# Nine propagation steps of a graph network: one panel in seven summed from rows fetched by index

## The chip, the core and the metric

One core of a Trainium2 chip runs the kernel: TensorE (PE) multiplies, VectorE (DVE), ScalarE (ACT) and GpSimd (POOL) work on tiles, and SyncE (SP) issues most DMAs, which run on 16 DMA engines. The metric is the time of one execution in microseconds of device time; less is better. In the rows PEld is PE's load of a weight block, and a name with a q behind it (SPq, PEq) is an engine's sequencer.

## What is computed

Four graph layers on 6250 nodes with 96 features and 100,000 edges (src, dst): attention, a softmax sum, ten steps of propagation (APPNP) and two graph convolutions. The change touches the third:

```python
# h: [6250, 96]; w = rsqrt(deg(src) * deg(dst)) for each edge
def spmm(feat):
    msg = feat[dst] * w[:, None]
    return segment_sum(msg, src, num_segments=6250)
out = h
for _ in range(10):
    out = spmm(out) * 0.9 + h * 0.1
```

## The kernel before

Nodes are cut into 49 tiles of 128. Once, in the attention stage, the kernel builds the adjacency as counts of edges, one byte (fp8) each, and stores it in HBM both ways round: `adjacency` and `adjacency_t`. For a tile of nodes (by src), a *panel* is its 128 columns of counts against all 6250 nodes (by dst), 49 blocks of 128 x 128 (128 rows of 6400 bytes). The sum for one tile is 49 matmuls (L1795), each with a block of counts as weights and 192 columns moving: 96 of the features in f16 and 96 of their remainder, so that the result is near f32. The features live in SBUF in two arrays, Ua (shown as `y`) and Ub (`u2b`), one read in a step and the other written.

A step has 7 *bodies* of 7 panels. Panel r of a body sits in ring slot r and sums into PSUM bank r. The queues:

- **SP** (`loads`, L1783) loads panel r of the next body as soon as PE is done with panel r of this one (`done`), so loads run a whole body ahead.
- **PE** (`products`) waits for the bank (`free`) and the slot (`ring_in`), then does 49 matmuls. In a step's first panel it waits before block 42 until all 49 tiles of this step's features are there (`u_ready`), so the last seven tiles of the step before may still be under way.
- **DVE** and **ACT** (`rows`, `copies`) turn each bank into the next features: ACT L1819, DVE L1804 and L1807, ACT L1822, DVE L1811, ACT L1825, each waiting for the one before.
- **POOL** does nothing in this stage.

The first step and the four pairs of steps after it are loops over bodies, the last step is unrolled. In the last step's first body the DVE also makes `w_squares`, for which PE waits (L1740).

Ahead of it lies the softmax layer (`softmax_dense`), whose 7 blocks of 7 panels are summed by L1443 with 385 columns. There DVE first makes the inputs (`product`, `remainders`, seven times) and then, block by block, empties the banks (L1521 and L1522, then the division L1529 to L1539). PE starts on a bank of the next block when DVE has emptied it.

The lists behind the counts: in the bucket stage edges are sorted to `k.slots`, for each group of 256 nodes by dst (25 groups) and each tile by src there are 128 slots, each of which holds at most one edge. Four planes hold src's position in the tile (plus one; zero for an empty slot) and three parts of dst's place in the group.

Of the kernel before, what the change touches and what calls it, by code (L numbers as in the profile page):

```python
# [5 lines left out]
ALU = mybir.AluOpType  # L6
# [34 lines left out]
BODIES = TILES // RING  # L41
SLOT = RING * BANK * GROUP
# [82 lines left out]
def signals(k):  # L125
# [17 lines left out]
    k.codes, k.decoded, k.planes = k.sig("codes"), k.sig("decoded"), k.sig("planes")  # L143
    k.base1, k.full_s, k.full_ps, k.filled_s = (k.sig(x) for x in ("base1", "full_s", "full_ps", "filled_s"))
# [809 lines left out]
def attention_and_adjacency(k, ctx):  # L954
# [392 lines left out]

    norm = Norm(k)
    vector(), gpsimd(), paired(pe, tensor_step), scalar(), paired(sp, sync_step, SP_LAG)
    for e in (v, a, pe, pool, sp):  # L1350
        for b in range(2):
            e.wait_ge(k.col_out[b].sem, k.col_out[b].at(PAIRS - 1 if b < last_tiles else PAIRS - 2, 15))
# [24 lines left out]
def dense_signals(k):  # L1377
    k.ring_in = [k.sig(f"ring{r}") for r in range(RING)]
    k.used, k.free, k.done = k.sig("used", RING - 1), k.sig("free", RING), k.sig("done", RING)
    k.w2_set, k.unit_root, k.shrunk = (k.sig(x) for x in ("w2_set", "unit_root", "shrunk"))  # L1380
# [8 lines left out]
    k.unit, k.unit_ps, k.per_unit = (k.sig(x) for x in ("unit", "unit_ps", "per_unit"))  # L1389
    k.x_out = k.sig("x_out")  # L1390

# [83 lines left out]

def softmax_dense(k, ps, bank, Y, Ua):
# [5 lines left out]
    with ExitStack() as ctx:  # L1482
# [7 lines left out]
        blocks = Blocks(k, ps, [U], cols)  # L1490
        folded = Folded(k, bank, k.T, k.wl[0:1], k.agg,
# [5 lines left out]
        def vector():  # L1497
# [15 lines left out]
            k.res.base += BODIES  # L1513
            for i in range(BODIES):
                v.wait_ge(k.agg.sem, k.agg.at(i))
# [135 lines left out]
        scalar(), vector(), scalar_sums(), tensor(), blocks.sync(early=1), first_loads()  # L1651
        for x in (v, a, k.pool):
            x.wait_ge(k.u_ready.sem, k.u_ready.at(TILES))
# [108 lines left out]
def appnp_and_convolutions(k, ctx, ps, bank, Ua, out):  # L1762
# [4 lines left out]
    v, a, pe, sp = k.v, k.a, k.pe, k.sp  # L1767
# [11 lines left out]
    def loads(n):  # L1779
        for r in range(RING):  # L1780
            sp.wait_ge(k.done.sem, k.done.at(RING * n["at"] + r + 1 - RING))
            k.settle(sp)
            sp.dma_start(k.ring[r][:, 0:WIDE], k.t_d[RING * n["body"] + r, :, :]).then_inc(k.ring_in[r].sem, 16)  # L1783

    def products(n):
        for r in range(RING):
            pe.wait_ge(k.free.sem, k.free.at(RING * n["at"] + r + 1 - RING))
            pe.wait_ge(k.ring_in[r].sem, k.ring_in[r].at(16 * n["at"] + 16))
            k.settle(pe)
# [36 lines left out]

    def numbers(eng):


        def bodies(step, U, Un, first=0):  # L1830
            if eng is pe:
                pe.wait_ge(k.u_ready.sem, k.u_ready.at(TILES * step + TILES - RING))
                k.settle(pe)
            with eng.Fori(first, BODIES) as i:
                yield {"step": step, "body": i, "at": step * BODIES + i, "this": U, "next": Un}
# [499 lines left out]
```

## Time and profile before

| | |
|---|---|
| median of 3 runs | 3998.27 us (3998.01 to 3999.06) |
| profiled execution, first to last instruction | 3998.4 us |
| PE busy | 3854.9 us, 96% |
| DVE, ACT, POOL busy | 44%, 33%, 15% |
| mean granted TensorE clock | 0.989 |
| propagation, L1795 from its loops on | 1594.4 to 3561.2 us |
| DMA engines, 2000 to 2200 us | 0.60 of their time, 204 GB/s |

The profile comes from one execution that was recorded; its span is the number in the second row, and what lies around it does not show beside the runs (0.1 us). A matmul's mean time in groups (246 ns) is its time in a pipeline; how fast they follow each other is read from a chain's length over its count.

### The profile page before, as it was taken

What the parts mean: (1) busy time and instruction counts of PE and PEld (TensorE: products, weight loads), DVE (VectorE), ACT (ScalarE), POOL (GpSimd) and SP (SyncE); (2) the same over time, 40 slices, a digit from 0 to 9 for tenths busy, and PEclk for the clock granted to TensorE, in tenths of its full rate; (3) what the DMA queues carried; (4) which work ended last, traced back from release to release, by engine and by line L of the source; (5) the groups of instructions that cost most, each with busy time, mean ns of one, the idle gap of its engine ahead of it and who ended that gap; (6) DMA issues with size and microseconds to landing.
All of it is one profiled execution on the core that took longest, in us unless ns stands there. A gap on an engine that the chain in (4) does not pass through costs nothing.

```text
span 3998.4 us, 124106 instructions
## 1 busy us (share of the span) xinstructions
PE 3854.9 (96%) x46183; PEld 3660.9 (92%) x46183; DVE 1769.7 (44%) x4393; ACT 1314.9 (33%) x3901; POOL 586.7 (15%) x714
## 2 busy tenths in 40 slices
PE   3889999999989999999999999999999998999999
PEld 2679999999956667999999999999999998999999
DVE  8999999999973324222222222222222222331111
ACT  1248888888871111222222122222222221111110
POOL 1016666666630000000000000000000000000000
PEclk9989999999989999999999999999999999999999
DMA  1039999889963333665665665656656665667775
GB/s 41 3 79 235 232 238 233 233 235 237 231 189 111 111 111 111 220 202 202 205 204 201 203 204 203 200 203 205 201 201 204 204 200 177 202 219 213 209 214 156
DMA packets 438001, 747.73 MB, mean 187 GB/s; under 512 B 197331, under 2 KB 330579, under 8 KB 437840
## 3 DMA queue, kind: packets, MB, share of 16 engines
q1 hardware_dynamic: 433346, 744.61, 61.1%
q8 instruction: 126, 2.06, 0.2%
q10 hardware_dynamic: 4494, 0.77, 0.1%
q14 instruction: 35, 0.29, 0.0%
HBM read 621.82 MB, written 83.32 MB: 176 GB/s over the span
## 4 chain that ended last, share of the span: by engine, by line
PE 91%; DVE 6%; ACT 1%; issue 1%; DMA 0%; ACTq 0%; DVEq 0%; SPq 0%; POOL 0%; POOLq 0%
PE sum L1795 49%; PE sum L1443 19%; PE pk L1182 10%; PE pr L1205 7%; PE pq L1194 3%; PE pc L1218 2%; DVE onerank L799 2%; PE l L475 1%; DVE bt L771 1%; DVE prodb L788 1%; DVE vals L781 1%; PE l L459 0%; DMA X<-in_x_dram 0%; DVE H L283 0%; PE sum L1622 0%
## 5 line engine op out<-in xcount | busy, mean ns | idle before, releaser
L1795 PE MATMUL sum<-u2b,ring 128*128 128x192 f16 x12005 | 994.1, 246 | 0.0
L1795 PEld LDWEIGHTS sum<-u2b,ring 128*128 128x128 fp8e4 x12005 | 993.1, 98 | 0.3
L1795 PE MATMUL sum<-y,ring 128*128 128x192 f16 x11662 | 962.9, 246 | 0.0
L1795 PEld LDWEIGHTS sum<-y,ring 128*128 128x128 fp8e4 x11662 | 962.2, 98 | 0.0
L1804 DVE TENSOR_TENSOR z<-lo,sum 128x96 f32<-128x96 f32 x441 | 112.2, 254 | 983.1 <-ACT lo L1819 982.8
L1182 PE MATMUL pk<-kv,hT 128*128 128x192 f16 x4900 | 485.6, 246 | 2.0 <-DVE hT L1074 2.0
L1443 PE MATMUL sum<-u,ring 128*128 128x385 f16 x2401 | 404.6, 329 | 12.4 <-ACT u L1585 12.4
L1182 PEld LDWEIGHTS pk<-kv,hT 128*128 128x128 f16 x4900 | 409.9, 99 | 2.4 <-DVE hT L1074 2.3
L1443 PEld LDWEIGHTS sum<-u,ring 128*128 128x128 fp8e4 x2401 | 236.0, 98 | 174.2 <-issue 13.6
L1264 ACT ACTIVATE kvs<-pk 128x384 f32<-128x384 f32 x735 | 301.0, 437 | 112.5 <-PE pk L1182 92.0
L1819 ACT ACTIVATE lo<-sum 128x96 f32<-128x96 f32 x441 | 110.1, 250 | 649.3 <-PE sum L1795 648.9
L1205 PE MATMUL pr<-wv,hs_wide 128*128 128x101 f32 x2450 | 321.2, 278 | 1.6 <-POOL wv L1135 1.6
L1130 POOL TENSOR_SCALAR sc<-sc,bound 128x20 f32<-128x20 f32 x245 | 270.2, 1103 | 276.5 <-DVE sc L1058 276.5
L1205 PEld LDWEIGHTS pr<-wv,hs_wide 128*128 128x128 f32 x2450 | 292.8, 192 | 1.9 <-POOL wv L1135 1.9
L1135 POOL TENSOR_TENSOR wv<-kvs,wv 128x480 f32<-128x480 f32 x245 | 246.5, 1006 | 204.2 <-DVE hd L1105 150.1
L1443 PE MATMUL sum<-u2b,ring 128*128 128x192 f16 x2401 | 203.0, 246 | 0.7 <-ACT u2b L1981 0.7
L1443 PE MATMUL sum<-y,ring 128*128 128x192 f16 x2401 | 202.2, 246 | 0.0
L1443 PEld LDWEIGHTS sum<-u2b,ring 128*128 128x128 fp8e4 x2401 | 199.1, 98 | 1.1 <-ACT u2b L1981 1.0
L1443 PEld LDWEIGHTS sum<-y,ring 128*128 128x128 fp8e4 x2401 | 199.0, 98 | 0.1
L1237 ACT ACTIVATE row<-pc 128x512 uint16<-128x512 f32 (+1 forms) x343 | 185.8, 546 | 0.7
L1254 ACT ACTIVATE hs_wide<-hs 128x640 f32<-128x640 bf16 x245 | 180.0, 735 | 0.0
L1051 DVE TENSOR_TENSOR qk<-pq,kvs 128x480 f32<-128x480 f32 x245 | 160.1, 653 | 42.9 <-ACT kvs L1264 42.9
(254 smaller groups left out, 3363.3 us busy)
## 6 DMA issues: line engine op xcount, KB each, us to landing
ring<-adjacency_t SPq DMA_DIRECT2D x490, 800.0 KB, 4.3
ring<-adjacency SPq DMA_DIRECT2D x147, 896.0 KB, 4.9
rows<-slot_rows_d SPq DMA_DIRECT2D x249, 320.0 KB, 4.0
adjacency<-row SPq DMA_DIRECT2D x49, 800.0 KB, 4.4
adjacency_t<-col SPq DMA_DIRECT2D x49, 800.0 KB, 4.6
col<-row SPq DMA_TRANSPOSE x245, 4.1
out_dram<-X SPq DMA_DIRECT2D x6, 336.0 KB
slot_rows_d<-T SPq DMA_DIRECT2D x2, 240.0 KB
```

The costliest lines, as they stand in the source:

```text
L1051: v.tensor_tensor(qk[i][:].rearrange("p (g d) -> p g d", d=D), pq[i][:, 0:CHUNK * D].rearrange("p (g d) -> p g d", d=D), kv[i][:, :, 0:D], ...
L1130: pool.tensor_scalar(sc[i][:], sc[i][:], k.bound[:, 0:1], k.bound[:, 1:2], ALU.min, ALU.max).then_inc(k.clipped.sem, 1)
L1135: pool.tensor_tensor(wv[i][:, :, 0:D].rearrange("p g (h d) -> p g h d", d=DH), kv[i][:, :, D:2 * D].rearrange("p g (h d) -> p g h d", d=DH ...
L1182: t = pe.matmul(pk[n][:, place:place + 2 * D], hT[i][:, 1 + m, g, :], k.kv[:, 2 * (g0 + g) + m, part, :], start=m == part == 0, stop=m == ...
L1194: t = pe.matmul(pq[i][:, g * D:(g + 1) * D], hT[i][:, 0, g, :], q2[b][:, part, :], start=part == 0, stop=part == 1)
L1205: t = pe.matmul(pr[:, 0:AV], hs_wide[e % HOMES][:, g, :], wv[i][:, g, :], start=g0 + g == 0, stop=g0 + g == GROUPS - 1)
L1237: a.activation(flat(row[b][:, g:g + count, :]), pc[u % 2][:, 0:count * P], ACT.Copy, accum_out=rowsum[:, bass.ds(X * (2 * UP) + u, 1)]).th ...
L1254: a.activation(flat(hs_wide[e % HOMES][:]), hs[e % 2][:].rearrange("p g a t -> p (g a t)"), ACT.Copy).then_inc(k.wide.sem, 1)
L1264: a.activation(flat(kv[i][:, 2 * n:2 * n + count, :]), pk[n][:, 0:count * 2 * D], ACT.Copy).then_inc(k.kv_out.sem, 1)
L1443: t = pe.matmul(self.ps[j][:, 0:self.cols], w[:, q, (j + odd) // 2, :, (j + odd) % 2], U[:, r * RING + q, 0:self.cols], start=r == q == 0, ...
L1795: m = pe.matmul(ps[r][:, 0:2 * D], w[:, t // 2, :, t % 2], n["this"][:, t, 0:2 * D], start=t == 0, stop=t == TILES - 1)
L1804: v.tensor_tensor(z[:, j, :], lo[:, j, :], ps[j][:, 0:D], ALU.add).then_inc(k.free.sem, 1)
```

## The change

For panel 6 of each body, in steps 2 to 10, the 49 blocks of counts are replaced by 25 pairs of a list and a one-hot. For each group of 256 nodes there is a list of 128 node numbers (`k.index`), one a slot, and a matrix of 128 slots by 128 columns that is 1 where the slot's edge belongs (`hots_d`, 3200 bytes a row). PE then does 25 matmuls (L1898 of the new kernel) with the one-hots as weights and the fetched rows moving. The rows, 128 of 384 bytes for each list, are fetched by GpSimd with one indirect DMA a list from a table of the features in HBM (`u_d`, one for each of Ua and Ub), into two buffers `got` in turn. What was added for it:

- SP stores the slots to HBM (`slots_d`) before attention.
- In the softmax stage POOL reads the planes back, works out the indices (`indices`) and stores one-hots (`store`), which DVE builds (`one_hots`), seven of 3200 elements, before it empties the first banks.
- In propagation SP stores each body's new features to the table (`publish`) behind the next body's loads, and POOL waits for all seven stores of a step before its first gather.
- The loops over bodies on SP, PE and POOL become one loop over four pairs of steps with 14 bodies written out; DVE's and ACT's stay.

```diff
+        sp.dma_start(k.slots_d, k.slots[:].rearrange("p i t g -> p (i t g)")).then_inc(k.slots_kept.sem, 16)
...
+    def one_hots(self, j):
+        v.wait_ge(k.listed.sem, k.listed.at(2))
+        for b in range(j * BODIES, (j + 1) * BODIES):
+            if b >= 2:
+                v.wait_ge(k.hot_out[b % 2].sem, k.hot_out[b % 2].at(16 * (b // 2)))
+            v.tensor_tensor(self.hots[b % 2][:], under(k.count1[:], GROUPS), over(self.which[:, b, :], P),
+                            ALU.is_equal).then_inc(k.hot_built.sem, 1)
+    def store(self):
+        for b in range(PICKED_TILES):
+            pool.wait_ge(k.hot_built.sem, k.hot_built.at(b + 1))
+            pool.dma_start(k.hots_d[b, :, :], flat(self.hots[b % 2][:])).then_inc(k.hot_out[b % 2].sem, 16)
...
+            if r >= PICKED and n["turn"]:
+                sp.dma_start(k.ring[r][:, 0:GROUPS * P], k.hots_d[(r - PICKED) * BODIES + n["body"], :, :]).then_inc(k.ring_in[r].sem, 16)
...
+    def publish(at, rows_of, h, b):
+        sp.wait_ge(k.u_ready.sem, k.u_ready.at(TILES + RING * at + RING))
+        sp.dma_start(k.u_d[h][RING * b * P:RING * (b + 1) * P, :].rearrange("(t p) d -> p t d", p=P),
+                     rows_of[:, tiles_of(b), 0:2 * D]).then_inc(k.u_out[h].sem, 16)
+    def gathers(n):
+        if b == 0:
+            pool.wait_ge(k.u_out[n["table"]].sem, k.u_out[n["table"]].at(16 * BODIES * n["times"]))
+        for j in range(PICKS):
+            h, at = (PICKS * n["turn"][0] + j) % 2, j * BODIES + b
+            pool.wait_ge(k.done.sem, k.done.at(RING * (n["at"] - 2 // PICKS) + PICKED + j + 1))
+            for g in range(GROUPS):
+                pool.indirect_dma_start(got[h][:, g, :], None, k.u_d[n["table"]], bass.IndirectOffsetOnAxis(
+                    ap=k.index[:, at, g:g + 1], axis=0)).then_inc(k.got[h].sem, 16)
...
+            if r >= PICKED and n["turn"]:
+                pe.wait_ge(k.got[turn % 2].sem, k.got[turn % 2].at(16 * GROUPS * (seen + turn // 2 + 1)))
+                for g in range(GROUPS):
+                    m = pe.matmul(ps[r][:, 0:2 * D], w[:, g, :], got[turn % 2][:, g, :],
+                                  start=g == 0, stop=g == GROUPS - 1)
```

On PE, two bodies in the last step read as follows before, each bank `sum_r` with its ring slot:

```order
L1795 MATMUL sum_4<-u2b,ring_4 128x192 x49
L1795 MATMUL sum_5<-u2b,ring_5 128x192 x49
L1795 MATMUL sum_6<-u2b,ring_6 128x192 x49
L1795 MATMUL sum_0<-u2b,ring_0 128x192 x49
L1795 MATMUL sum_1<-u2b,ring_1 128x192 x49
```

And in the change, in the unrolled pair of steps:

```order
L1908 MATMUL sum_4<-u2b,ring_4 128x192 x49
L1890 REGISTER_ALU
L1908 MATMUL sum_5<-u2b,ring_5 128x192 x49
L1890 REGISTER_ALU
L1894 ISA
L1898 MATMUL sum_6<-got0,ring_6 128x192 x25
L1890 ISA
L1891 ISA
L1908 MATMUL sum_0<-u2b,ring_0 128x192 x49
```

The seventh bank takes 25 matmuls from `got0` (then `got1`) in place of 49 from the features in SBUF. On POOL, whose program had no row for this stage, the loop now begins so, the gathers of body 0 and body 1 of a step:

```order
L2006 UNCONDITIONAL_BRANCH
L2006 ISA
L1882 ISA
L1885 DMA got0<-u_rows_d1,index 128x192 x25
L1882 ISA
L1885 DMA got1<-u_rows_d1,index 128x192 x25
```

Between two bodies' gathers stands only the wait for a buffer. On DVE, at the end of the softmax layer's inputs, before:

```order
L1566 TENSOR_TENSOR T<-T,u1 128x672
L1568 TENSOR_TENSOR y1<-y1,u1 128x672
L1521 TENSOR_TENSOR dn1<-lo1,sum_0 128x192
L1522 TENSOR_SCALAR ideg<-sum_0 128x1
L1521 TENSOR_TENSOR dn1<-lo1,sum_1 128x192
```

and in the change:

```order
L1644 TENSOR_TENSOR T<-T,u1 128x672
L1646 TENSOR_TENSOR y1<-y1,u1 128x672
L1533 TENSOR_TENSOR hots0<-count1,which 128x3200
L1533 TENSOR_TENSOR hots1<-count1,which 128x3200
L1533 TENSOR_TENSOR hots0<-count1,which 128x3200
L1533 TENSOR_TENSOR hots1<-count1,which 128x3200
L1533 TENSOR_TENSOR hots0<-count1,which 128x3200
L1533 TENSOR_TENSOR hots1<-count1,which 128x3200
L1533 TENSOR_TENSOR hots0<-count1,which 128x3200
L1599 TENSOR_TENSOR dn1<-lo1,sum_0 128x192
L1600 TENSOR_SCALAR ideg<-sum_0 128x1
```

Seven comparisons now stand between the last remainder and the first sum.

## Rows read from the trace of the kernel before

**Rows 1.** The page: the chain that ended last, shares by line.

```profile
PE sum L1795 49%; PE sum L1443 19%; PE pk L1182 10%; PE pr L1205 7%; PE pq L1194 3%; PE pc L1218 2%; DVE onerank L799 2%; PE l L475 1%; DVE bt L771 1%; DVE prodb L788 1%; DVE vals L781 1%; PE l L459 0%; DMA X<-in_x_dram 0%; DVE H L283 0%; PE sum L1622 0%
```

**Rows 2.** Chain in order of time: start us, length us, what.

```profile
1594.39 1782.75 PE sum L1795 x21609
3388.70 172.48 PE sum L1795 x2058
```

**Rows 3.** Windows: PE, PEld, DVE, ACT, POOL busy; granted clock; DMA share; GB/s.

```profile
2000.00:2200.00 200.00, 200.00 (x2427) 200.00 (x2425) 41.00 (x148) 40.53 (x149) 0.00 (x0) 1.00 0.60 204
```

**Rows 4.** Timeline of ACT, one panel sum and the next: start us, length us.

```profile
2200.80 0.25 ACT L1819 ACTIVATE lo<-sum 128x96 f32<-128x96 f32 x1 [1.52 <-PE sum L1795]
...
2203.03 0.28 ACT L1825 ACTIVATE y<-r 128x96 f32 x1 [0.70 <-DVE r L1811]
2204.84 0.25 ACT L1819 ACTIVATE lo<-sum 128x96 f32<-128x96 f32 x1 [1.53 <-PE sum L1795]
```

**Rows 5.** Chain at the start of the last step.

```profile
3377.23 0.26 ACT lo L1888
...
3387.95 0.74 PE l L1740 x2
```

**Rows 6.** Windows behind that idle stretch: PE busy, clock, DMA share, GB/s.

```profile
3390.00:3395.00 5.00, 5.00 (x38) 0.59 0.01 3
3395.00:3400.00 5.00, 5.00 (x64) 1.00 0.48 164
```

**Rows 7.** Line 1783, the ring loads: ns min/median/max on SP, us to landing.

```profile
L1783 SPq DMA_DIRECT2D ring<-adjacency_t x483: 327/333/343, 1587.7 to 3533.0; - x161
...
DMA to landing us min/median/max: 4.0/4.3/11.7
```

**Rows 8.** DMA list of the whole span: the smallest loads.

```profile
es<-in_src_dram SPq DMA_DIRECT2D x25, 18.0 KB, 1.7
```

**Rows 9.** Lines by form, GpSimd: count, busy us, mean ns.

```profile
L1135 POOL TENSOR_TENSOR wv<-kvs,wv 128x480 f32<-128x480 f32 x245 | 246.5, 1006 | 204.2 <-DVE hd L1105 150.1 <-ACT wv L1244 51.1 <-issue 0.2
```

**Rows 10.** Line 1130 on GpSimd: ns min/median/max.

```profile
L1130 POOL TENSOR_SCALAR sc<-sc,bound x245: 352/1537/1540, 273.6 to 1126.1; 128x20 f32<-128x20 f32 x123
```

**Rows 11.** DMA in propagation, 2000 to 2200 us: packets, MB, share of 16 engines.

```profile
q1 hardware_dynamic: 7149, 40.74, 60.3%
```

**Rows 12.** DMA in attention, 300 to 330 us.

```profile
DMA packets 7796, 7.23 MB, mean 241 GB/s; under 512 B 6206, under 2 KB 6206, under 8 KB 7792
...
q1 hardware_dynamic: 7792, 7.18, 95.4%
```

**Rows 13.** Timeline where the softmax sums begin, 1189 to 1262 us.

```profile
1191.64 32.58 PE L1443 MATMUL sum<-u,ring 128*128 128x385 f16 x196 [0.20 <-ACT u L1585]
...
1194.50 0.86 DVE L1566 TENSOR_TENSOR T<-T,u 128x672 f32<-128x672 f32 x1
...
1195.39 0.86 DVE L1568 TENSOR_TENSOR y<-y,u 128x672 f32<-128x672 f32 x1
...
1201.61 0.35 DVE L1521 TENSOR_TENSOR dn<-lo,sum 128x192 f32<-128x192 f32 x1 [5.35 <-ACT lo L1597]
...
1205.40 0.36 DVE L1529 TENSOR_SCALAR e<-dn 128x384 f32<-128x384 f32 x1
...
1209.83 0.56 DVE L1539 TENSOR_TENSOR T<-dn,H 128x384 f32<-128x384 f32 x1
```

**Rows 14.** Lines by form, VectorE: the comparison that builds bt.

```profile
L771 DVE TENSOR_TENSOR bt<-number,tiles 128x1764 bf16<-128x1764 bf16 x25 | 26.8, 1071 | 0.0
```

**Rows 15.** Timeline at 1141 us, while GpSimd works too.

```profile
1131.90 10.63 POOL L1340 TENSOR_TENSOR X<-X,T 128x672 f32<-128x672 f32 x6
...
1140.99 2.25 DVE L1566 TENSOR_TENSOR T<-T,u 128x672 f32<-128x672 f32 x1
```

**Rows 16.** Chain after 3600 us, where PE runs unrolled code.

```profile
3612.02 16.17 PE sum L1443 x196
```

**Rows 17.** Instruction DMA from 3600 to 3998 us: packets, MB, share.

```profile
q8 instruction: 39, 0.64, 0.6%
```

More of the change, by code:

```diff
@@ L1379, in dense_signals @@
     k.used, k.free, k.done = k.sig("used", RING - 1), k.sig("free", RING), k.sig("done", RING)
-    k.w2_set, k.unit_root, k.shrunk = (k.sig(x) for x in ("w2_set", "unit_root", "shrunk"))
+    k.w2_set, k.unit_root, k.shrunk = Again(k, k.counted, GROUPS), Again(k, k.before, GROUPS), Again(k, k.same, 2 * GROUPS)
     k.u_set, k.exps, k.prods, k.hi, k.res, k.lo, k.hi2, k.res2, k.lo2 = (
@@ L1651, in softmax_dense @@
         scalar(), vector(), scalar_sums(), tensor(), blocks.sync(early=1), first_loads()
+        picked.indices(), picked.store(), picked.end()
         for x in (v, a, k.pool):
@@ L1762, in appnp_and_convolutions @@
 def appnp_and_convolutions(k, ctx, ps, bank, Ua, out):
-    v, a, pe, sp = k.v, k.a, k.pe, k.sp
+    v, a, pe, pool, sp = k.v, k.a, k.pe, k.pool, k.sp
+    got = [k.buf(ctx, f"got{i}", [P, GROUPS, 2 * D], F16) for i in range(2)]
     Ub = k.buf(ctx, "u2b", [P, TILES, 2 * D], F16)
@@ L1850, in last_products, with sync, publish_before, gpsimd @@
                 unit.sums()
+    def sync():
+        for b in range(1, BODIES):
+            loads({"body": b, "at": b, "turn": None})
+            publish(b - 1, Ub, 1, b - 1)
+        with sp.Fori(0, last // 2) as s:
+            for n in pair(s):
+                loads(n)
+                publish_before(n)
+        for n in last_each():
+            loads(n)
+            if n["body"] == 0:
+                publish_before(n)
+    def publish_before(n):
+        h, b = n["table"], n["body"]
+        if b == 0:
+            publish(n["at"] - 1, n["this"], h, BODIES - 1)
+        else:
+            publish(n["at"] - 1, Ua if n["this"] is Ub else Ub, 1 - h, b - 1)
+    def gpsimd():
+        with pool.Fori(0, last // 2) as s:
+            for n in pair(s):
+                gathers(n)
+        for n in last_each():
+            gathers(n)
     def last_rows():
-        for n in last_numbers():
+        for n in last_each():
             b = n["body"]
@@ L1880, in last_copies @@
     def last_copies():
-        for n in last_numbers():
+        for n in last_each():
             b = n["body"]
@@ L1896, in last_copies @@
                 unit.root()
-    for n in numbers(sp):
-        loads(n)
-    for n in numbers(pe):
-        products(n)
+    sync(), tensor(), gpsimd()
     for n in numbers(v):
@@ L1905, in appnp_and_convolutions @@
         copies(n)
-    for n in last_numbers():
-        loads(n)
-    last_products(), last_rows(), last_copies()
+    last_rows(), last_copies()
     of_all = STEPS * BODIES
@@ L2016, in dense_layers @@
         Ua = Y[:].bitcast(F16)
+        k.index = k.buf(ctx, "index", [P, PICKED_TILES, GROUPS], I32)
         ps, bank = [k.bank(ctx, f"sum_{j}") for j in range(RING)], k.bank(ctx, "l")
```

116 lines of the change are left out of this document (99 added, 17 removed).

## Prediction

> **What bounds the kernel now.** I read the chain of work that ended last first. Propagation's matmul line L1795 alone is 49% of the span, the largest item by far [rows 1]. The chain in order of time then shows 21,609 of its matmuls in 1782.75 us without a piece of anything else between them [rows 2]. That is 82.5 ns a block, 4.04 us for a panel of 49 blocks, 28.3 us for a body and 198.1 us for a step. A window of 200 us inside has PE and its weight loads busy for all 200, VectorE and ScalarE for 41 each, GpSimd for nothing, and the DMA engines for 0.60 of their time [rows 3]. So every block taken from PE there is worth 82.5 ns, as long as nothing that PE needs comes later than PE.
>
> Two things are to be seen beside that. The work behind a panel is a chain on ScalarE and VectorE: it starts at 2200.80, its last copy ends at 2203.31, and the next begins at 2204.84 when the next panel is done [rows 4]. It is 2.51 us of 4.04, so it has slack. And PE's only idle stretch in propagation is in the last step, from 3377.2 to 3387.95 [rows 5]. After it the granted clock is 0.59 in the window from 3390 to 3395, where 38 matmuls ran, and 1.00 in the next, where 64 did [rows 6]: the lower level, 1.2 GHz, and then 2.4 again. The 2058 matmuls behind the gap took 172.48 us, 83.8 ns each, and 169.8 would have done [rows 2]. So a wait of 10.7 us cost another 2.7 us in clock.
>
> **The change, part by part.** Removed: in 63 bodies (nine steps of seven) the seventh panel needs 25 blocks in place of 49. 63 x 24 x 82.5 ns = 124.7 us, or 13.9 us a step. This is certain; the rest eats from it.
>
> Added in each step, the gathers. They read a table in HBM that holds all 49 tiles, so none of a step's gathers can start before the last tile of the step before is copied, stored and landed. Let S be the moment when PE ends a step. Panel 5 ended 2.06 us (25 blocks) earlier, its chain of 2.51 us ends at S + 0.5, that of panel 6 at S + 3.1 [rows 4]. (PE needs these tiles at block 42 of the next panel, S + 3.5: still in time, with 0.4 us left where there was 0.9.) SP issues the store in 0.33 us, and I let it land like a ring load, whose least is 4.0 us [rows 7]: S + 7.5. GpSimd starts at S + 7.6. The 25 gathers of body 0 take 25c, c being the time that GpSimd needs for one, and the last lands 1.7 us after its issue, as the smallest loads do [rows 8]. PE, meanwhile, has six full panels, 24.3 us. So PE waits 7.6 + 25c + 1.7 - 24.3 = 25c - 15.0 us at body 0's seventh panel. For the seventh body the same account is 7.6 + 175c + 1.7 - (24.3 + 6 x 26.3) = 175c - 172.8, since gathers run on behind each other, two bodies deep. PE's wait in a step is the larger of the two. They cross at c = 1.05.
>
> No row shows c. From below it is SP's issue of a load to 128 partitions, 0.33 us [rows 7]; from above a whole small load from issue to landing, 1.7 us, as if no two overlapped [rows 8]. I take 1.0 us: a software engine builds addresses for 128 partitions here, and the nearest row on that engine is its two-input operation, 1006 ns [rows 9]. It could be disturbed: another GpSimd instruction takes 352 ns at best and 1537 at the median beside a busy VectorE [rows 10], but VectorE is busy only a fifth of the time in propagation [rows 3]. At c = 1.0 the wait is 10.0 us, and by the gap above 2.7 us of clock come with it: 12.7 a step, 114.3 us in nine.
>
> The SBUF page of the Trainium skill (SBUF — State Buffer, SBUF: two separate sides) gives about 620 ns for a GpSimd-issued DMA alone, and 3100 ns beside a VectorE operation that holds the shared port. By the first figure as an estimate for c the wait would be 0.5 us and the kernel at about 3905; no run here shows it, and it is a plain DMA, not one that reads indices. The second figure would be the rival of a GpSimd that is the bound, and is kept out by the code, where propagation's VectorE operations take two inputs.
>
> DMA load: a body's 3200 fetched rows of 384 bytes and 896 stored ones. A packet of the ring loads takes 0.27 us of an engine (0.603 x 16 x 200 us over 7149 [rows 11]). In attention 7792 packets, 6206 of them under 512 bytes, took 458 engine-us in 30 us [rows 12]. If the 1586 others cost 0.27 each, 0.005 us is left for a small one; if all cost the same it is 0.059. With 0.059 the rows add 242 us to the 421 that 16 engines have in a body of 26.3, 0.57 on top of the rings' 0.60: over the limit. In proportion to bytes (384 of 6400) a row costs 0.02, which adds 0.19. I take this one, between the ends and in keeping with the bytes, at no cost to PE, and keep the other as a rival.
>
> Added once, the one-hots. Seven comparisons of 3200 elements stand on VectorE between the last remainder, which ends at 1196.25, and the first sum at 1201.61 [rows 13]. At one element a cycle (384 elements 0.56 us, 672 elements 0.86: 1.04 ns each [rows 13]) one is 3.5 us; at the rate of the bf16 comparison, 1764 in 1.07 us [rows 14], 1.8. I take 3.5, the output being bytes. Two buffers, and a store that lands about 5 us after a buffer is built (GpSimd's 1.0 and 4.0 as above): the pace becomes 8.5 us a pair, and VectorE is free after 28.9 us, at 1225.2. PE needs bank 0 at 1207.8, two panels of 8.1 us behind 1191.64 [rows 13]. It gets it at 1225.7: 17.9 us. Bank 4 waits behind four sums and the 5 us of division that begin at 1205.40 in the trace of before [rows 13]: 2.6 us more. With 2.7 of clock: 23.2. Bounds: 4 (1.8 us each and no wait for stores) and 30. PE is the bound all through this stage, so nothing gives it back.
>
> Small ones. The slots' store, 1.28 MB, goes in front of SP's queue where attention begins and the engines are busiest: 0 to 3.5 us, I take 1.8. The index arithmetic on GpSimd falls under the chain on which PE waits there; beside GpSimd one VectorE operation took 2.25 us [rows 15] in place of 0.86 [rows 13], so 2 us. PE's loop is now 14 unrolled bodies. Unrolled code runs at 82.5 ns as well, 196 matmuls in 16.17 us [rows 16], while 39 instruction fetches pass [rows 17]; the branch back comes at a step's start, under the wait for gathers. Nothing for it; up to 10 us if that cover is gone.
>
> **Sum** against the profiled execution, whose span of 3998.4 us is within 0.2 of the median of 3998.27: 3998.4 - 124.7 + 114.3 + 23.2 + 1.8 + 2.0 = **4015 us**, +0.4%.
>
> **The rivals.** With F = 3900.7 for all but the gathers, the time is F + 9 x (wait + 2.7).
>
> *Gathers are cheap (c below 0.89): faster.* The place is body 0's seventh panel and the price 225 us per microsecond of c. At c = 0.8 the wait is 5.0: 3970. At 0.6 it is gone: 3901. It decides from c = 0.93, where the sum is nil. For it: GpSimd's small operation takes 352 ns undisturbed [rows 10] and SP's issue 333 [rows 7]. Against: those do no address work in software. Chance 0.36. The Trainium skill's figure of 620 ns, cited above, stands on this side.
>
> *GpSimd becomes the bound (c above 1.06): slower by 1% and more.* At 1.1 the seventh body waits 19.7: 4102. At 1.2, 37.2: 4260. At 1.7, 124.7: 5048. For it: the 1537 ns in [rows 10], and that 25 gathers must fit in 26.3 us with nothing over. Chance 0.23.
>
> *The DMA engines become the bound.* At a load of 1.17 a body takes 30.8 us, 2.5 more than before: 3998.4 + 27.0 + 63 x 2.5 = 4183. For it: the 95% in [rows 12]. Against: ring loads there and here are large packets with room beside them [rows 3]. Chance 0.04.
>
> *My forecast*, c from 0.89 to 1.06: 3990 to 4040. Chance 0.37. It rests on a GpSimd instruction over 128 partitions being worth a microsecond, as in [rows 9].
>
> **How the numbers follow.** About 0.2%, 8 us, is what a measurement of this kernel can tell from no change. Faster is c below 0.89: 0.36. Within 8 us is c from 0.89 to 0.96, a wait of 7.2 to 9.0 us: 0.12. The rest is slower, 0.52. The range leaves out c above 1.17 (4213) and keeps the case without any wait: 3900 to 4215. The forecast's own range is 3990 to 4040.
>
> **What would show it.** Right: line L1898's matmuls, 1575 of them, with PE idle some 10 us before those of body 0 of each step, released by the gathers, almost nothing before the other six, a clock of about 0.6 behind each wait, gathers a microsecond apart on GpSimd, and a PE gap near 1208 us of some 18 us. Wrong: PE waiting at every seventh panel (GpSimd too slow), a step of 184 us without a gap (c small), or waits at L1908 for ring loads (DMA full). The prediction is most sensitive to c: 0.1 us of it is 22 us of time, and above 1.05, 157.

## The result, and the profile of the changed kernel

The changed kernel takes 5836.84 us (5834.33 to 5838.57), the kernel before 3998.18 us in the same comparison: a ratio of 1.460, interval 1.458 to 1.462. The prediction was 4015 us with a range from 3900 to 4215. The profiled execution has a span of 5836.9 us at a mean granted clock of 0.82.

The page of the changed kernel: the shares of the chain that ended last by engine and by line (answers to [rows 1]), and the costliest groups.

```profile
PE 67%; issue 27%; DVE 5%; ACT 1%; DMA 0%; ACTq 0%; DVEq 0%; SPq 0%; POOL 0%; POOLq 0%
PE sum L1908 36%; PE sum L1456 12%; PE pk L1186 7%; PE pr L1209 5%; PE sum L1898 2%; PE pq L1198 2%; PE pc L1222 1%; DVE onerank L803 1%; PE l L479 1%; DVE bt L775 0%; DVE prodb L792 0%; DVE vals L785 0%; DVE hots L1533 0%; PE l L463 0%; DMA X<-in_x_dram 0%
...
L1885 POOL DMA_INDIRECT got<-u_rows_d,index x1575 | 1495.2, 949 | 2634.5 <-PE sum L1898 1131.9
L1908 PE MATMUL sum<-u2b,ring 128*128 128x192 f16 x10290 | 1085.6, 262 | 846.6 <-issue 845.3
...
L1908 PE MATMUL sum<-y,ring 128*128 128x192 f16 x10290 | 1033.3, 258 | 691.1 <-issue 690.4
```

What the reader expects after the prediction, PE waiting for fetched rows at L1898, isn't there at all. In its place PE stands idle for 1536 us in front of the matmuls of the six *other* panels, and what ended that time is "issue": it waited for nothing that the profile shows. It is GpSimd that waits for PE. The timeline of PE, one body and the start of the next (L1908: a panel of counts; L1898: the fetched panel), shows the form of it:

```profile
2444.14 2.23 PE L1898 MATMUL sum<-got,ring 128*128 128x192 f16 x25
2446.20 5.72 PE L1908 MATMUL sum<-y,ring 128*128 128x192 f16 x66
2452.17 0.24 PE L1908 MATMUL sum<-y,ring 128*128 128x192 f16 x1 [0.25 <-issue]
...
2469.15 0.32 PE L1908 MATMUL sum<-y,ring 128*128 128x192 f16 x1 [1.08 <-issue]
2471.25 0.32 PE L1908 MATMUL sum<-y,ring 128*128 128x192 f16 x1 [1.78 <-issue]
2473.35 0.32 PE L1908 MATMUL sum<-y,ring 128*128 128x192 f16 x1 [1.78 <-issue]
...
2482.48 18.89 PE L1908 MATMUL sum<-y,ring 128*128 128x192 f16 x200 [1.08 <-issue]
2501.21 2.23 PE L1898 MATMUL sum<-got,ring 128*128 128x192 f16 x25
```

When PE ends L1898 at 2446.2, GpSimd starts the next 25 gathers (one body's 25 in a row are called a *burst* here). PE runs 66 more matmuls at full speed, and then from 2452 to 2482 it issues few: first three or four at a time, then single ones, 0.7 to 2.1 us apart in this body, until the burst is over. Then 200 follow in 18.9 us. A body takes 57.1 us (2444.14 to 2501.21) in place of 26.3. I call this a *slow phase*. Windows of the changed kernel, with the columns of [rows 3]: 200 us of propagation, a piece between bursts and one within a burst.

```profile
2000.00:2200.00 200.00, 130.28 (x1363) 118.57 (x1363) 24.44 (x89) 23.80 (x89) 67.35 (x72) 0.78 0.46 140
2427.00:2446.00 19.00, 19.00 (x220) 18.88 (x219) 3.90 (x14) 3.80 (x14) 0.00 (x0) 0.94 0.56 181
2454.00:2474.00 20.00, 4.42 (x19) 1.74 (x19) 0.86 (x3) 0.82 (x3) 15.12 (x17) 0.56 0.33 81
```

1363 matmuls in 200 us stand against 2427 before. In the burst there are 19 in 20 us, the DMA engines are two thirds idle, and the clock has fallen to 0.56. The gaps come before the fall: from 2446 to 2452 the granted clock is 1.00, and the matmul at 2452.17, behind the first gap, still lasts 0.24 us; those from 2469 on last 0.32. So the low clock doesn't start the slow phase.

### The profile page after: what moved, and what is told of

Same layout as the page of the kernel before. It is cut to its first block, busy times and chain, and to the rows that moved or that the text cites. A ratio compares the mean times of both kernels' runs of the same rounds, so it can differ in the third digit from the quotient of the medians.

```text
span 5836.9 us, 121842 instructions
## 1 busy us (share of the span) xinstructions
PE 4137.6 (71%) x44671; PEld 3658.3 (63%) x44671; DVE 1793.2 (31%) x4400; ACT 1313.7 (23%) x3901; POOL 2074.9 (36%) x2311
## 4 chain that ended last, share of the span: by engine, by line
PE 67%; issue 27%; DVE 5%; ACT 1%; DMA 0%; ACTq 0%; DVEq 0%; SPq 0%; POOL 0%; POOLq 0%
PE sum L1908 36%; PE sum L1456 12%; PE pk L1186 7%; PE pr L1209 5%; PE sum L1898 2%; PE pq L1198 2%; PE pc L1222 1%; DVE onerank L803 1%; PE l L479 1%; DVE bt L775 0%; DVE prodb L792 0%; DVE vals L785 0%; DVE hots L1533 0%; PE l L463 0%; DMA X<-in_x_dram 0%
## 5 line engine op out<-in xcount | busy, mean ns | idle before, releaser
L1885 POOL DMA_INDIRECT got<-u_rows_d,index x1575 | 1495.2, 949 | 2634.5 <-PE sum L1898 1131.9
L1908 PE MATMUL sum<-u2b,ring 128*128 128x192 f16 x10290 | 1085.6, 262 | 846.6 <-issue 845.3
L1908 PEld LDWEIGHTS sum<-u2b,ring 128*128 128x128 fp8e4 x10290 | 921.5, 103 | 1006.1 <-issue 995.6
L1908 PE MATMUL sum<-y,ring 128*128 128x192 f16 x10290 | 1033.3, 258 | 691.1 <-issue 690.4
L1908 PEld LDWEIGHTS sum<-y,ring 128*128 128x128 fp8e4 x10290 | 904.0, 102 | 816.2 <-issue 808.1
L1456 PE MATMUL sum<-u,ring 128*128 128x385 f16 x2401 | 405.9, 329 | 29.9 <-DVE ideg L1600 16.5
L1134 POOL TENSOR_SCALAR sc<-sc,bound 128x20 f32<-128x20 f32 x245 | 235.6, 962 | 285.2 <-DVE sc L1062 285.2
L1456 PE MATMUL sum<-u2b,ring 128*128 128x192 f16 x2401 | 203.0, 246 | 0.7 <-ACT u2b L2136 0.7
L1456 PE MATMUL sum<-y,ring 128*128 128x192 f16 x2401 | 202.2, 246 | 0.0
L1456 PEld LDWEIGHTS sum<-u2b,ring 128*128 128x128 fp8e4 x2401 | 199.1, 98 | 1.1 <-ACT u2b L2136 0.9
L1456 PEld LDWEIGHTS sum<-y,ring 128*128 128x128 fp8e4 x2401 | 199.0, 98 | 0.1
```

Source lines behind the costliest of these rows:

```text
L1134: pool.tensor_scalar(sc[i][:], sc[i][:], k.bound[:, 0:1], k.bound[:, 1:2], ALU.min, ALU.max).then_inc(k.clipped.sem, 1)
L1456: t = pe.matmul(self.ps[j][:, 0:self.cols], w[:, q, (j + odd) // 2, :, (j + odd) % 2], U[:, r * RING + q, 0:self.cols], start=r == q == 0, ...
L1885: pool.indirect_dma_start(got[h][:, g, :], None, k.u_d[n["table"]], bass.IndirectOffsetOnAxis(ap=k.index[:, at, g:g + 1], axis=0)).then_in ...
L1908: m = pe.matmul(ps[r][:, 0:2 * D], w[:, t // 2, :, t % 2], n["this"][:, t, 0:2 * D], start=t == 0, stop=t == TILES - 1)
```

## The experiments

Eighteen runs were made, of seventeen kernels, each beside the kernel before. The letters of the theories hold within one batch only; each is told where it first stands. "The change" in an expectation is the changed kernel. The edits are shown in part; `...` marks what is left out.

**First batch: which part of the change does it.** Two parts were added to the kernel before, alone and together: gathers that nobody reads (20 a body, of 128 neighbouring rows), and PE's code of steps 2 to 9 written out body by body, as the change has it. The fourth is the change without its gathers. The edit of the gathers and that of the fourth:

```
+    def fetch(at, turn, seen):
+        h = turn % 2
+        pool.wait_ge(k.done.sem, k.done.at(RING * (at - 2) + RING))
...
+        for g in range(20):
+            pool.indirect_dma_start(got[h][:, g, :], None, k.u_table, bass.IndirectOffsetOnAxis(
+                ap=index[:, g:g + 1], axis=0)).then_inc(k.got[h].sem, 16)
+        pool.wait_ge(k.got[h].sem, k.got[h].at(16 * 20 * (seen + turn // 2 + 1)))
...
-            for g in range(GROUPS):
-                pool.indirect_dma_start(got[h][:, g, :], None, k.u_d[n["table"]], ...
+            pool.memset(got[h][:, 0:1, 0:2], 0.0).then_inc(k.got[h].sem, 1)
```

Gathers beside PE's loop:

> The kernel before with GpSimd gathers beside it: 20 indirect DMAs of 128 rows of 384 bytes for each body of steps 2 to 10, paced by the same signal as in the change, and read by nobody; PE keeps its loop over one body and all its 49-block panels. Theory A (PE's instruction fetch does not get through while GpSimd runs gathers; code that loops in place needs none): 3998 to 4015 us, PE at 82.5 ns a block. Rival B (gathers slow PE itself, by SBUF or semaphore traffic): PE falls back in each burst of 25 us as in the change, above 5000 us. Rival C (the DMA engines are too busy, ring loads land late): PE waits for ring loads at L1795, 4050 to 4400 us.

PE's code written out, no gathers:

> The kernel before with PE's loop written out to 14 bodies, as the change has it, and no gathers. Theory A: code that is only run straight on is fetched in time, so 3998 to 4010 us, with a microsecond or so for each of the three branches back. Rival D (unrolled PE code is slow in itself in this stage): PE drops to single matmuls as in the change, above 5000 us. B and C: no change, 3998 us.

Both:

> Both together: PE's loop written out to 14 bodies and the 20 gathers a body beside it, still read by nobody. Theory A: PE loses most of each burst (20 gathers at 1.25 us are 25 us, of which some 20 are lost): 4900 to 5400 us, with single matmuls 1 to 2.5 us apart and no 16 KB instruction packet inside the bursts. Rival B and C: the same time as the run with gathers and the looped code. Rival D: the same time as the unrolled code alone.

The change without its gathers:

> The change with its gathers left out: GpSimd only counts its semaphore up, and PE multiplies the one-hots with a buffer of zeros, so that a seventh of the sums is left out. Everything else stays: stores to the table, one-hots, slots, unrolled code. It measures all terms of the prediction but the gathers: 3900.7 us by its sum. Theory A: 3895 to 3915. If PE's unrolled code or the new stores were what costs, it stays above 4500.

Measured: 4004.43 us (ratio 1.0013, 1.0003 to 1.0022) for gathers beside the loop; 4008.55 (1.0024, 1.0014 to 1.0034) for written-out code; 4019.71 (1.0050, 1.0034 to 1.0066) for both; 3915.27 (0.9789, 0.9773 to 0.9806) for the change without gathers. So every theory that blamed the mere pair of gathers and written-out code seemed to fall. It had not: these four ran on chip 1, on which no kernel had slow phases, and in the third batch a pair of the same kind (47 of its rows are row 64) has them on chip 14. What stays is that the change without its gathers, which leaves a seventh of the sums out, is 83 us faster than the kernel before.

**Second batch: the rows.** The lists have empty places (some 46 of 128), and all of a list's empty places name one row. Perhaps these reads of one row disturb. The edits: `k.index` from an iota (rows in order, so that the seventh panels sum other rows); `part` plus (row p - 64) times (place is empty) (own rows); PE's steps 2 to 9 as a loop with one buffer `got`; and the run with both parts, with 47 of its 128 rows the same.

> The change as it is, but every gather takes 128 neighbouring rows of the table (group g the rows from 128g) in place of the rows that the lists name, so the seventh panels sum other rows than the reference. Theory H (in the change about 46 of a list's 128 places are empty and all name one row, and these reads of one row hold up the fetching of TensorE's written-out instructions): the single matmuls 0.7 us apart vanish, GpSimd's 25 x 1.25 us a body bound the steps, 3915 + 9 x 48.7 = about 4353 us (4300 to 4450). Theory S (what slows TensorE is not in the rows but in the rest of the change: SyncE's and GpSimd's code written out beside TensorE's, or TensorE's wait on the fetched rows): as the change, 5837 us (5700 to 5900). Theory R (any rows that aren't in order, not one row above all): as H here.

> The change with one thing more: each empty place of a list names a row of its own (row p of the group's 256) in place of the one that all of them name; its factor in the one-hots is zero, so the sums stay what they are. Theory H (the reads of one row): about 4353 us (4300 to 4450). Theory R (rows out of order): 5837 us (5700 to 5900), since 82 of 128 rows are scattered as before. Theory S: 5837 us.

> The change with TensorE's code of steps 1 to 8 as a loop over bodies again and one buffer of fetched rows in place of two (a loop can't name them in turn). The burst for a body now begins when the seventh panel before it is done and the panel waits for its landing: a body is 31.25 + 2.7 landing + 2.1 for the 25 matmuls = 36.3 us, against 26.3 of TensorE alone, so 3915 + 63 x 10 = about 4550 us (4450 to 4700) under every theory that puts the slow matmuls down to fetching written-out instructions (H, R, and S as far as it is TensorE's own code); the last step, still written out, may be slow by itself (+150). If TensorE is slow for another reason (power, the reading of the fetched rows, banks): each of the 294 matmuls of the six panels is as slow as now, and a body is 31 + 26 us or more: 5840 us and up.

> The kernel before with TensorE's steps written out and 20 gathers a body beside them that nobody reads (the earlier run of this kind took 128 neighbouring rows and 4020 us): now 81 of a gather's 128 rows are every third of 256, and the other 47 are one row, as in the lists of the change. Theory H: TensorE's fetches are held up for the 25 us of each 28 that gathers run, over 4900 us. Theory R: the same, over 4900. Theory S: 4020 us (4010 to 4040).

Measured: rows in order 4314.07 us (1.079, 1.0772 to 1.0808), own rows 4315.72 (1.0787, 1.0769 to 1.0805), the loop with one buffer 4735.13 (1.1839, 1.1819 to 1.1859), one row in 47 places 4020.13 (1.0052, 1.0036 to 1.0069). The first three were free of slow phases, so theory H looked confirmed; but the fourth, which should have shown it, was free of them too. H was in doubt, and the third said that the change's own rows did no harm beside a loop.

**Third batch: which row.**

```
-    pool.tensor_scalar(place[:], place[:], 243.0, 1.0, ALU.min, ALU.mult)
+    # in words: row 3p up to place p = 81, else row 64 (six instructions)
...
-        pool.iota(self.own[:], [[0, GROUPS]], base=-P // 2, channel_multiplier=1, ...
+        pool.memset(self.own[:, 0:GROUPS - 1], 179.0).then_inc(k.listed.sem, 1)
```

> As the run with TensorE's steps written out, 20 gathers that nobody reads and 47 of 128 rows the same (4020 us), but the one row is row 64 of the group's 256, the very row that the change's empty places name, in place of row 243. Theory A (it matters where in memory the one row lies): TensorE waits for its instructions as in the change, over 4500 us. Theory B (the rows alone don't do it; it takes something else of the change with them, such as the stores of the table, SyncE's written-out code or TensorE's wait for the fetched rows): 4020 us (4010 to 4030).

> The change, but the empty places name row 243 of their group (in the last group row 123) in place of row 64; still one row for all of a list's empty places. Theory A (where the one row lies): 4316 us, as with a row for each place (4300 to 4500). Theory B (that it is one row, together with something else of the change): 5837 us (5700 to 5900).

> The change, but of the empty places those above 104 name row 65 and those below row 64, so that some 23 places name one row in place of 46. If the number of reads of one row in one gather matters and each costs its time, the slow phases get shorter: about halfway between 4316 and 5837, 5000 us (4600 to 5500). If there is a threshold: 4316 or 5837.

Measured: 5431.71 (1.3579, 1.3556 to 1.3602), 5815.12 (1.4537, 1.4513 to 1.4562) and 5808.7 (1.4524, 1.4499 to 1.4548). The two rows, expected at 5000 if the number of reads counts, cost as much as one. Neither theory explains all three together with the batch before: row 243 is harmless in one kernel (4020) and not in another (5815). What this batch did give is the effect without the rest of the change: slow phases beside gathers that nobody reads. Windows from 2000 to 2200 us of the run with row 243 and of that with row 64:

```profile
2000.00:2200.00 200.00, 196.75 (x2353) 196.10 (x2351) 39.82 (x144) 39.16 (x144) 128.48 (x136) 0.98 0.75 232
```

```profile
2000.00:2200.00 200.00, 129.84 (x1313) 114.46 (x1311) 21.99 (x80) 21.77 (x80) 75.29 (x80) 0.78 0.42 131
```

**Fourth batch: loop, nine rows, row 127.** The same edits with PE's loop restored, with `own = p / 6 - 13.667`, and with 127 for 64.

> The run with 47 of 128 rows at row 64 that took 5432 us, but TensorE's steps 1 to 8 as the kernel before has them, a loop over bodies; the gathers are the same and nobody reads them. Theory F (what these reads hold up is the fetching of TensorE's written-out instructions): the slow phases vanish in steps 1 to 8, about 4015 us; the last step has its own written-out code and may keep its slow phases (up to 7 x 25 = 175 us more, 4190). Theory G (TensorE's matmuls or its reading of memory are slowed themselves): about 5430 us as with written-out steps.

> The change, but the some 46 empty places of a list name nine neighbouring rows (64 to 72 of the group, about six places each) in place of one. If only many reads of the very same row do it: 4316 us, as with a row for each place. If it is that these places all name rows close together: 5837 us. Two rows of 23 each gave 5809 us. I expect something between, near 4316 (4300 to 5000).

> As the run with TensorE's steps written out and the same row 64 in 47 of 128 places of 20 gathers that nobody reads (5432 us), but the one row is 127 of the group. With row 243 it was 4020 us. If row 243 was spared because of where it lies, any other row may be slow or not: 4020 or about 5430. If row 243 was spared because it was the row that follows the last of the listed ones (3 x 81), so that the reads never go back: 5430 us here, since row 127 lies below the last.

Measured: 5465.42 (1.3668, 1.3645 to 1.3691), 5835.45 (1.4594, 1.4569 to 1.4618), 5467.68 (1.3674, 1.3651 to 1.3697). The nine rows, expected near 4316, missed. The first is the important one. PE's code is the loop of the kernel before, and the slow phases are there at the same size (the expectation of Theory G). From 2000 to 2200 us the DMA list of that run has 2 packets in the queue `q8 instruction`, that of the run with written-out code and row 64 has 11 for about as many matmuls (1276 against 1313), so the loop isn't fetched anew in each turn. Theory F, that fetching of written-out code is held up, fell. GpSimd's first gather and PE in that kernel, from the panel's end that released the burst:

```profile
2105.45 0.95 POOL L1936 DMA_INDIRECT got<-u_rows_d,index  x1 [27.45 <-PE sum L1799]
```

```profile
2104.74 5.47 PE L1799 MATMUL sum<-u2b,ring 128*128 128x192 f16 x64
2110.48 0.24 PE L1799 MATMUL sum<-u2b,ring 128*128 128x192 f16 x1 [0.27 <-issue]
...
2120.50 0.32 PE L1799 MATMUL sum<-u2b,ring 128*128 128x192 f16 x1 [1.81 <-issue]
2123.28 0.32 PE L1799 MATMUL sum<-u2b,ring 128*128 128x192 f16 x1 [2.47 <-issue]
...
2133.78 22.70 PE L1799 MATMUL sum<-u2b,ring 128*128 128x192 f16 x254 [1.78 <-issue]
```

**Fifth batch: a version meant to win.** Own rows; body 0 of a step takes counts throughout, and bodies 1 to 6 fetch 22 lists and keep the last five blocks of counts, so that GpSimd's 6 x 22 x 1.25 us fit into a step. The second has PE's bodies 1 to 6 as a loop of pairs.

```
+                for g in range(LISTS):
+                    m = pe.matmul(ps[r][:, 0:2 * D], w[:, g, :], got[turn % 2][:, g, :], start=g == 0, stop=False)
...
+                for t in range(2 * LISTS, TILES):
+                    m = pe.matmul(ps[r][:, 0:2 * D], w[:, t // 2, :, t % 2], n["this"][:, t, 0:2 * D],
+                                  start=False, stop=t == TILES - 1)
```

> A version that should beat both: a row for each empty place; in six of a step's seven bodies (not the first, which would wait for the whole table) 22 of the 25 lists are fetched and the five last blocks of counts stay. GpSimd needs 22 x 1.25 = 27.5 us for a body and has seven bodies' time (about 188 us) for six; the last burst ends at about 6.5 + 165 + 2.7 = 174 us of a step, TensorE comes to it at 185: no wait. Saved: 54 x 22 x 82.5 ns = 98.0 us, against 124.7 in the run without gathers (3915 us), and the gathers beside written-out code cost 11 us in an earlier pair of runs: 3915 + 26.7 + 8 = about 3950 us (3935 to 3975). If GpSimd still binds: over 4000.

> The same with TensorE's bodies 1 to 6 of a step as a loop over pairs of bodies (the two buffers in turn), its first body written out. If fewer instructions to fetch are worth what the kernel before's steps written out cost (10 us): about 3942 us (3930 to 3965). If the loop of two bodies (642 matmuls and as many loads) is fetched anew in each turn, the same as written out, 3950.

Measured: 5374.37 (1.3438, 1.3416 to 1.3461) and 5378.34 (1.3447, 1.3425 to 1.3469): both missed, with slow phases in both, though no two empty places share a row. With this, no rule by rows was left.

**The two last: rows against code, and chip against kernel.** The kernel with own rows again, with one constant changed (`base=0, channel_multiplier=0`), so that instruction for instruction it is the 4316 us kernel and fetches the rows of the 5837 us kernel:

> The kernel with a row for each empty place (4316 us), instruction for instruction, but one constant is other: the empty places all name row 64 of their group again, so that the gathers fetch exactly the rows that the change fetches (5837 us), by the code of the kernel that took 4316. Theory R (the rows that are fetched decide): 5837 us (5750 to 5850). Theory P (the rows are all the same to it, and what decides is something that a few instructions more or less on GpSimd ahead of the gathers shift): 4316 us (4300 to 4350).

Measured: 4332.2 us (1.0838, 1.082 to 1.0856), free of slow phases. The rows don't decide. Theory P, the placing of GpSimd's code, would remain, but it doesn't sort the runs either: counted in GpSimd instructions ahead of the first gather, the change plus 0, 1, 4 and 5 gave slow, free, free, slow, and plus 0 (the loop with one buffer) free, plus 4 (22 lists) slow. Nor does the place of the buffers: the version with row 243 (5815, slow) allocates the same buffers as the own-rows kernel (4316, free). What does sort them is the chip that timed them, and the last run asked for that with the kernel of 5374 us:

> The version with 22 lists (5374 us, timed on chip 9), the same kernel once more. Theory C (what slows TensorE during bursts of gathers goes with the chip, not with the kernel: all kernels with gathers timed on chips 1 and 11 were free of it, all timed on chips 9 and 14 had it, whatever their rows and code): on chip 1 or 11 3950 us (3935 to 3975), below the kernel before; on chip 9 or 14 5374 us; on another chip one of these two. Theory K (it goes with the kernel): 5374 us on every chip.

Measured: 5375.41 us (1.3438, 1.3416 to 1.3461), on chip 10, one not used so far: as Theory K has it, and as Theory C has it too, so this run doesn't tell them apart. All runs with gathers by chip:

```
chip  1: 4004 (loop, rows in order)  4020 (written out)  4332 (own-rows code, one row)      free
chip 11: 4314 (in order)  4316 (own rows)  4735 (loop, one buffer)  4020 (row 243)          free
chip 14: 5432 (row 64)  5815 (row 243)  5809 (two rows)  5465 (loop)  5835 (nine)  5468     slow
chip  9: 5374 (22 lists)  5378 (22 lists, loop)                                             slow
chip 10: 5375 (22 lists)                                                                    slow
```

The kernel before took 3998 to 4000 us on every one of them. Chips 9, 10 and 11 timed one batch each, chips 1 and 14 two each. The chip that timed the change isn't known.

## Why the prediction was wrong

There is a trace of the change without slow phases too, from chip 1: the own-rows code with one row fetches the same rows with the same instructions behind four small ones. With it, the prediction's error, 5836.8 - 4015 = 1821.8 us, splits in three:

| part | predicted | measured | error |
|---|---|---|---|
| all but the gathers (F) | 3900.7 | 3915.3 | +14.6 |
| waits for the gathers, with their clock | 114.3 | 416.9 (4332.2 - 3915.3) | +302.6 |
| PE slow beside the gathers | 0 | 1504.6 (5836.8 - 4332.2) | +1504.6 |

The third row is a difference between runs on chip 1 and on a chip that isn't known, by kernels four small instructions apart. So two steps failed. The larger is the overlap: "PE, meanwhile, has six full panels, 24.3 us", put at 82.5 ns a block whatever GpSimd does. In the changed kernel these six panels take 55.0 us (2446.20 to 2501.21). The smaller is the size of c. The parts in turn:

**The removed blocks: right.** In the run without gathers a step is 184.2 us (PE's next step starts at 1967.94, this one at 1783.71) against 198.1 in [rows 2]: 13.9 a step, 124.7 in all, as predicted.

**What was added once: the predicted mechanism, but less of it.** PE waited for bank 0 until 1224.21 (predicted 1225.7) behind seven comparisons of 3.4 us (3.5 predicted) and the stores of their two buffers. The timeline of the changed kernel there:

```profile
1205.62 6.89 DVE L1533 TENSOR_TENSOR hots<-count,which 128x3200 uint8<-128x3200 bf16 x2 [2.90 <-DMA hots_d<-hots]
1213.43 10.29 DVE L1533 TENSOR_TENSOR hots<-count,which 128x3200 uint8<-128x3200 bf16 x3 [0.93 <-DMA hots_d<-hots]
1224.21 18.00 PE L1456 MATMUL sum<-u,ring 128*128 128x385 f16 x98 [16.52 <-DVE ideg L1600]
1612.23 27.97 PE L1908 MATMUL sum<-y,ring 128*128 128x192 f16 x337
```

Propagation starts at 1612.23, 17.8 us later than in [rows 2]; the prediction's terms for what stands ahead of it are 23.2 + 1.8 + 2.0 = 27.0. The wait for bank 0 is 16.5 us (17.9 predicted), bank 4 isn't waited for at all (2.6 predicted), and from 1191.32, where the sums begin no later than before (1191.64), the slots' store and the index arithmetic left no delay (3.8 predicted). Written-out code was put at nothing, up to 10 if its cover is gone, and without gathers the cover was gone. The run with it alone lost 8.7 us against the kernel before in the same batch (4008.6 - 3999.9), and PE stands there 2.9, 2.8 and 2.9 us at the three returns of the loop over pairs of steps. In the run without gathers it stands for 4.66 us at the first return, with 1.5 us of clock behind it, and 14.6 us at all three:

```profile
2150.10 2.23 PE L1896 MATMUL sum<-got,ring 128*128 128x192 f16 x25
2156.98 25.94 PE L1906 MATMUL sum<-u2b,ring 128*128 128x192 f16 x294 [4.66 <-issue]
```

So all but the gathers came to 3915 against F = 3900.7 by two errors that partly cancel: too much for what is added once, nothing for the returns. In the own-rows code with one row, where PE waits for gathers too, 6.0 us at the three returns are left.

**The smaller step that failed: c.** The prediction took 1.0 us for a gather, "a GpSimd instruction over 128 partitions being worth a microsecond". An instruction takes 0.95 us; but between two of them there are 0.30 us that the row in [rows 9] doesn't hold, since a mean duration isn't a period. The two gathers' rows, then PE at three bodies of a step in the same kernel without slow phases:

```profile
2021.96 0.94 POOL L1894 DMA_INDIRECT got<-u_rows_d,index  x1 [0.30 <-issue]
2023.21 0.95 POOL L1894 DMA_INDIRECT got<-u_rows_d,index  x1 [0.30 <-issue]
```

```profile
1824.31 4.16 PE L1907 MATMUL sum<-got,ring 128*128 128x192 f16 x25 [17.46 <-DMA got<-u_rows_d,index]
1828.27 25.23 PE L1917 MATMUL sum<-u2b,ring 128*128 128x192 f16 x294
1855.54 2.22 PE L1907 MATMUL sum<-got,ring 128*128 128x192 f16 x25 [2.05 <-DMA got<-u_rows_d,index]
...
2012.33 2.22 PE L1907 MATMUL sum<-got,ring 128*128 128x192 f16 x25 [1.19 <-DMA got<-u_rows_d,index]
...
2054.21 4.16 PE L1907 MATMUL sum<-got,ring 128*128 128x192 f16 x25 [15.41 <-DMA got<-u_rows_d,index]
```

c = 1.25 is above the crossing at 1.05, so in this kernel GpSimd is the bound: bodies follow at 31.3 us (1824.31 to 2012.33 is six of them), which is 25 x 1.25, and a step is 229.9 us (1824.31 to 2054.21). The prediction's own formula gives for c = 1.25 a wait of 175 x 1.25 - 172.8 = 46.0 us, a step of 184.2 + 48.7 = 232.9 us, and F + 9 x 48.7 = 4339 us. Measured: 229.9, and 4332 and 4316. So where PE isn't slowed the model of the step was right in its sum, and its rival "GpSimd becomes the bound" (chance 0.23, at 1.2 us 4260) is what happens. It was not right in how the sum is made up: PE waits before every fetched panel, 34.8 us in all in this step, and the other 10.9 us, not 2.7, are mostly the clock: behind five of a step's seven waits the 25 matmuls take 3.6 to 4.2 us in place of 2.2, and the granted clock from 2000 to 2200 us is 0.91. c had no row, and the value between the bounds was taken from the duration of another instruction. With c = 1.25 the range, which ended at c = 1.17, would have missed too.

The 620 ns of the Trainium skill for a GpSimd-issued DMA (SBUF — State Buffer, SBUF: two separate sides) stood on the cheap side. The row for a gather of 128 rows is 0.95 us busy and 1.25 us apart, the spacing twice that. The 3100 ns that the same section of the Trainium skill gives beside a VectorE operation, the prediction's other rival, didn't show: the longest of the changed kernel's 1575 gathers lasted 1.51 us.

**The larger step that failed: PE's pace beside the gathers.** No case in the prediction has PE slowed without waiting for anything, and no reason was given for putting it at nothing. The slow phases are 1505 of the 1839 us that the change loses, 23.9 us for each of 63 bursts. In the kernels that only add gathers to the one before it is the same: (5431.7 - 4020.1) / 63 = 22.4 and (5465.4 - 4004.4) / 63 = 23.2 us. So the price is nearly the burst itself, 25 to 31 us, in which PE does some 60 matmuls at its pace and then few.

Shown for them: they come only beside GpSimd's gathers (no run without gathers has one, and in the changed kernel the last body of each step, beside which no gather runs, has 26.3 us), from the first burst on and in every burst of a kernel that has them; they need neither written-out PE code (the loop has them) nor PE's use of the rows (rows that nobody reads have them) nor rows named many times (own rows have them); and gathers themselves are as fast with them as without (949 and 953 ns).

Not shown: the cause. That it goes with the chip rests on seven batches, three free and four slow, without an exception among sixteen runs with gathers. The rule was found by sorting the results afterwards, and one run, the last, was made on it. But no kernel was timed on both kinds of chip, the same kernel twice fell on slow ones, and the two nearest pairs (the change and the own-rows code with one row; gathers beside a loop, with rows in order and with row 64) differ in a few instructions or in rows as well. That it goes with something in the kernel that I haven't found isn't excluded. What PE's sequencer lacks in those phases the profile doesn't name.

**The other rivals.** DMA engines as the bound: no. In the kernel without slow phases no ring load was waited for, at a share of 0.71 against 0.60 in [rows 3]; there 18.0% of 16 engines' 200 us went to 152 gathers, 0.03 us a row, where 0.02 was taken. Where the slow phases are absent, gathers beside PE cost it little: 5 us beside the loop (4004.4 - 3999.9), 11 beside written-out code (4019.7 - 4008.6).

**The version with one buffer and the loop** was expected at 4550 and took 4735. A body is mostly 38.1 us (2103.14 to 2141.21 is one) and not 36.3: the 25 matmuls behind the wait take 4.1 us at the low clock and not 2.1. That is 113 us in 63 bodies. In 13 of the bursts GpSimd stands once for 3.6 to 7.4 us between two gathers and waits for nothing that the profile shows, which is 64 us more; the last row is one of them. Steps' first bodies, where the burst also waits for the table, take about 44 us, which the expectation left out too. Against that, the 3915 us that it starts from hold the returns of the written-out loop, some 19 us with their clock, which a loop over bodies doesn't have.

```profile
2107.09 24.61 PE L1908 MATMUL sum<-y,ring 128*128 128x192 f16 x294
2108.09 0.94 POOL L1885 DMA_INDIRECT got<-u_rows_d,index  x1 [7.36 <-PE sum L1898]
2141.21 4.06 PE L1898 MATMUL sum<-got,ring 128*128 128x192 f16 x25 [9.50 <-DMA got<-u_rows_d,index]
...
2151.10 0.94 POOL L1885 DMA_INDIRECT got<-u_rows_d,index  x1 [4.09 <-issue]
```

No version beat the kernel before. Whether 22 lists would on a chip without slow phases (3950 us was the estimate) isn't known.

## What to carry to other kernels

An instruction's mean duration is not the period at which an engine repeats it: before a plan is built on n of them in a row, look for a row that has two behind each other, or leave room for a gap; here 0.30 us on 0.95 moved the bound from TensorE to GpSimd. That an engine waits for nothing doesn't mean that it keeps its pace beside a new neighbour: time the pair first, with work that nobody reads. When experiments by parts contradict each other, sort them by what was not varied on purpose (here the chip and the batch) before the next theory by parts, and time the same kernel again early; I did so with the last run of eighteen. And a change that leans on GpSimd's software DMAs beside a TensorE-bound loop should be timed on more than one chip.

## What the runs showed of the hardware

- An indirect DMA of 128 rows of 384 bytes occupies GpSimd for 0.94 to 0.95 us and the next comes 1.25 us after it, whatever the rows: in order, scattered, or 47 times the same. In 13 of 63 bursts of the kernel with one buffer GpSimd stands 3.6 to 7.4 us between two of them.
- In slow phases TensorE first runs on for 64 to 66 matmuls from the end of the panel that releases the burst, in the changed kernel's written-out code as in the loop (64), and then issues few: groups of up to four, then single ones, mostly 0.7, 1.4, 2.1 or 2.8 us apart. ScalarE is late as well in places: in the loop kernel a copy at 2114.82 stands behind 7.61 us of idle time, where 1.53 is usual.
- The granted clock follows: 0.56 within a burst, 0.94 between bursts.
- A loop of 14 written-out bodies leaves TensorE without work where it returns: 4.7 to 5.0 us in the run without gathers (14.6 us in three returns), 2.8 to 2.9 us in the one with whole panels, 1.6 to 2.6 us where it waits for gathers in each body.
